# A top-2 expert layer on one core: tiles of two 128-slot halves, each with its own expert

## The chip, the core and the metric

The kernel runs on one core of a Trainium2 chip. The metric is the device time of one execution in microseconds (us). The engines are named as the profile names them: PE is TensorE, with its weight load as PEld, DVE is VectorE, ACT is ScalarE, POOL is GpSimd and SP is SyncE. A q behind a name (SPq, PEldq) is what that engine's sequencer does itself: register reads, waits, issues of DMAs.

## What is computed

The input x is 4 sequences of 1024 tokens of 128 numbers, all float32. Two blocks follow one another, each behind a layer norm with a shift, a scale and a gate drawn from a condition. The first is a scan over time: a small MLP is trained by one gradient step for each of 1024 time steps on all four sequences at once, and then applied to the queries. The second, which the change concerns, is a mixture of experts with 8 experts, 2 for each token, and a shared expert:

```python
def _L0_ffn_ref(x, w_router, W1, b1, W2, b2, Ws1, bs1, Ws2, bs2):
    D_MODEL, D_FF, N_EXPERTS, TOP_K, N_SHARED = (128, 512, 8, 2, 1)
    ...
    probs = jax.nn.softmax(logits, axis=-1)
    vals, idx = jax.lax.top_k(probs, TOP_K)
    gates = jnp.sum(jax.nn.one_hot(idx, N_EXPERTS, dtype=x.dtype) * vals[..., None], axis=-2)
    hs = jax.nn.gelu(jnp.einsum('btd,fd->btf', x, Ws1) + bs1)
    acc = jnp.einsum('btf,df->btd', hs, Ws2) + bs2
    h = jax.nn.gelu(jnp.einsum('btd,efd->btef', x, W1) + b1)
    y = jnp.einsum('btef,edf->bted', h, W2) + b2
    acc = acc + jnp.einsum('bted,bte->btd', y, gates)
    return SCALE * acc
```

## The kernel before

**Stages.** The scan (line 413 is the helper that records most of its matmuls) takes the first 345 us. From there to about 444 us come the queries, the second norm, the routing and the first 9 of 16 shared tiles. The rest, to about 620 us, is the stage of tiles. Last come the loads, sums and stores of the output.

**Tiles.** The 4096 tokens with 2 experts each make 8192 slots. They are sorted by expert into a DRAM array `xs` of 132-word rows (128 of the token, 4 of place and gate) by indirect DMAs that POOL issues. A tile is TS = 256 slots of one expert; since each expert's last tile may be part empty, the kernel runs the worst case, N_TILES = 39 tiles. DVE works out on the chip which expert tile j has (`e_i[j]`) and where it begins in `xs` (`row_i[j]`): for the first N_FULL = 9 tiles in `full_tiles`, from half of the routing alone, for the rest in `rest_marks`, `rest_experts` and `rest_rows` (lines 1832 to 1864). `table_ready` counts these tables.

**Jobs.** 39 expert tiles and the last 7 shared tiles make 46 jobs. In iteration i PE transposes the rows of job i+2 (`feed`, line 1424, 2 transposes), runs the first layer of job i+1 (`e_up`, line 1442, 4 matmuls of 256 columns into PSUM) and the second of job i (`e_down`, line 1456, 8 matmuls of 128 columns). A float32 matmul shows as two passes in the trace. ACT makes the gelu between the layers (line 1586, 4 instructions of 128x256). DVE copies the transposed rows out of PSUM (`hg`, line 1884), works out where each result row goes (`meta`, lines 1891 to 1897, 4 small operations), adds the bias (`yb`, line 1917) and multiplies by the gate (`yo`, line 1922). POOL writes `yo` to its places in DRAM (`ys`, line 2052).

**Loads.** SP issues both loads of a tile, in one queue: `weights(j)` brings both layers and biases of one expert (578 KB, `slab`, a ring of RW = 5) and waits until `yb` of tile j-5 is made; `rows(j)` brings the 256 rows (132 KB, `xt`, a ring of RX = 4). In the loop `weights(j)` follows `rows(j)`. At the turn to the later tiles SP waits for the second table, issues the weights of tiles 9 and 10, and only then the rows of tile 9. From tile LOAD_AT = 33 on it also issues the first loads of results, `yg`.

**End.** The output is finished in 8 groups of 512 tokens. `load(g)` brings a group's 512 KB of expert results; DVE sums it by three operations of 128x512 (`group_step`, lines 1871, 1874, 1878), and `store(g)` issues 4 stores. The eighth group is an exception: PE sums its two halves by matmuls with the identity (line 1531) and DVE needs two operations (lines 2012, 2016). SP stores the even groups, ACT the odd ones.

Of the kernel before, what the change touches and what calls it, by code (L numbers as in the profile page):

```python
# [10 lines left out]
I32 = mybir.dt.int32  # L11
# [20 lines left out]
SLAB = 2 * F + FT + D  # L32
N_TILES = (2 * B * S) // TS + E - 1
# [4 lines left out]
N_FULL = -(-(B * S - E * (TS - 1)) // TS)  # L38
EARLY_SH = 9
BY_HALF = -(-((B * S + E * (TS - 1)) // TS) * TS // TS)  # L40
BY_THREE = -(-((3 * B * S // 2 + E * (TS - 1)) // TS) * TS // TS)
# [8 lines left out]
XS_ROWS = -(-(E * CAP + (E - 1) * TS) // (8 * P)) * 8 * P  # L50
# [4 lines left out]
RW = 5  # L55
YS_ROWS = 2 * B * S + RY * TS
ROW = D + 4
N_TAB = E + E + E * E + CAP // TS + N_TILES + CH + SUB * RY + D


def program(nc, x, w_q, w_kv, w1, b1, w2, b2, w_router,
            s_w1t, s_b1, s_w2t, s_b2, cond, w_mod, slabs, ident_in, before_in, lower_in, tabs_in, xs, ys, out):
    with ExitStack() as ctx:
# [60 lines left out]
        etab = sb("etab", [P, N_TILES])  # L124
        e_i = sb("e_i", [P, N_TILES], I32)
        row_i = sb("row_i", [P, N_TILES], I32)
# [6 lines left out]
        for name, width in (("iota", E), ("down", E), ("tri", E * E), ("step", CAP // TS), ("tile", N_TILES), ("tau", CH), ("dump", SUB * RY), ("b2row", D)):  # L133
            cut[name] = tabs[:, at:at + width]
            at += width
# [1061 lines left out]
        with block() as blk:  # L1197
# [18 lines left out]
            over = psb("over", [P, E, CAP // TS])  # L1216
            tri = psb("tri", [P, 3 * E, E])
            past = psb("past", [P, N_FULL, E])
            full, number, weight = psb("full", [P, E]), psb("number", [P, 3 * E]), psb("weight", [P, 3 * E])
            first, rowf = psb("first", [P, N_TILES]), psb("rowf", [P, N_TILES])  # L1220
# [3 lines left out]
            slab = [psb(f"slab{i}", [P, SLAB]) for i in range(RW)]  # L1224
            hg = [psb(f"hg{i}", [P, TS]) for i in range(2)]
            hid = [psb(f"hid{i}", [P, FT, TS]) for i in range(2)]
# [3 lines left out]
            row2, rested = psb("row2", [P, SUB]), psb("rested", [P, 1408])  # L1230
# [19 lines left out]
            s_slab = [sem(f"s_slab{i}") for i in range(RW)]  # L1250
            meta_step, meta_ready = sem("meta_step"), sem("meta_ready")
            sum_ready, fin_ready, s_out = sem("sum_ready"), sem("fin_ready"), sem("s_out")
# [23 lines left out]
            def store(eng, g):  # L1276
                eng.wait_ge(fin_ready, g + 1)
                for b in range(B):
# [863 lines left out]
```

## Time and profile before

| What | Before |
|---|---|
| median of 3 runs | 635.91 us (635.18 to 636.79) |
| the profiled execution's own time | 635.87 us |
| span in its trace, first to last instruction | 634.1 us |
| mean granted TensorE clock | 0.967 |
| busy in the span: PE, PEld, DVE, ACT, POOL | 570.1, 512.1, 443.8, 333.6, 391.1 us |
| first layer of the expert tiles, L1442 | 312 passes, mean 380 ns |
| second layer, L1456 | 624 passes, mean 275 ns |
| weights of a tile, issue to landing | 39 loads of 578.0 KB, median 3.8 us |
| rows of a tile, issue to landing | 39 loads of 132.0 KB, median 3.2 us |
| results of a group, issue to landing | 8 loads of 512.0 KB, median 6.7 us |

The span leaves out 1.8 us of the execution's time. A pass of PE is listed with a duration that overlaps the next pass; how far the starts of passes are apart is read from the timeline. Idle time of an engine counts only where another engine waits for it.

### The profile page before, as it was taken

To read this page: it belongs to the slowest core of one execution; us is meant where nothing else is said; L and a number is where in the kernel's file an instruction comes from. 1 tells how busy PE (TensorE), PEld (TensorE's weight loads), DVE (VectorE), ACT (ScalarE), POOL (GpSimd) and SP (SyncE) were. 2 spreads that over 40 slices of the span, in tenths; PEclk is the share of its full clock that TensorE was granted. 3 is DMA by queue.
4 is the path that set the end of the run, shared out by engine and by line. 5 is a ranking of instruction groups with operands and counts; after the bars stand their busy time and mean duration, and the time that the engine had idled before them with its cause. 6 is when DMAs were issued, how large, how long until landed. Compare 5 with 4: busy or idle time off the path is not lost. (4 is left out here: it accounts for less than half of the span.)

```text
span 634.1 us, 14426 instructions
## 1 busy us (share of the span) xinstructions
PE 570.1 (90%) x4296; PEld 512.1 (81%) x4296; DVE 443.8 (70%) x1743; ACT 333.6 (53%) x1064; POOL 391.1 (62%) x598
## 2 busy tenths in 40 slices
PE   2469999999999999999996868789979999999993
PEld 2349999899999999999985557778869999999991
DVE  3736888888788888878886478884595465555765
ACT  2555666566566666656662374775434444444440
POOL 1525666656666665666652607888888886677760
PEclk9999999999999999999999768879999999999997
DMA  9079930000000000000000001145445577778945
GB/s 198 3 275 394 395 136 1 2 0 0 0 0 0 0 0 0 0 0 0 2 2 1 2 0 35 46 143 168 143 137 147 177 222 225 227 239 256 347 123 165
DMA packets 39796, 66.77 MB, mean 105 GB/s; under 512 B 7522, under 2 KB 26724, under 8 KB 39748
## 3 DMA queue, kind: packets, MB, share of 16 engines
q1 hardware_dynamic: 31076, 54.85, 27.4%
q0 software_dynamic: 4544, 9.45, 4.3%
q10 hardware_dynamic: 4128, 1.91, 1.4%
q8 instruction: 22, 0.36, 0.2%
q14 instruction: 26, 0.21, 0.1%
HBM read 36.26 MB, written 29.92 MB: 104 GB/s over the span
## 5 line engine op out<-in xcount | busy, mean ns | idle before, releaser
L1586 ACT ACTIVATE hid<-bank,slab 128x256 f32<-128x256 f32 x156 | 64.1, 470 | 85.1 <-PE bank L1442 85.0
L2052 POOL DMA_INDIRECT ys<-yo,dst x78 | 76.3, 979 | 36.8 <-DVE yo L1922 22.2
L2044 POOL DMA_INDIRECT xs<-hrow,slot_i x64 | 63.4, 990 | 35.8 <-issue 35.5
L1442 PE MATMUL bank<-hg,slab 128*128 128x256 f32 x312 | 73.9, 380 | 4.3 <-issue 3.9
L1456 PEld LDWEIGHTS bank<-slab,hid 128*128 128x128 f32 x624 | 75.8, 192 | 2.0
L1456 PE MATMUL bank<-slab,hid 128*128 128x128 f32 x624 | 76.0, 275 | 0.0
L1442 PEld LDWEIGHTS bank<-hg,slab 128*128 128x128 f32 x312 | 56.3, 190 | 11.0 <-issue 4.9
L1917 DVE TENSOR_TENSOR yb<-bank,slab 128x256 f32<-128x256 f32 x39 | 16.6, 424 | 61.9 <-PE bank L1456 61.7
L990 POOL TENSOR_TENSOR nL<-aL,ones 128x128 f32<-128x128 bf16 x32 | 16.9, 527 | 42.5 <-ACT aL L699 42.5
L413 PE MATMUL bank<-aH,W2p 128*128 128x128 f32 x192 | 42.4, 303 | 0.1
L413 PE MATMUL bank<-kv,W1b 128*128 128x128 f32 x192 | 41.4, 298 | 0.0
L1002 POOL TENSOR_TENSOR nH<-aH,ones 128x128 f32<-128x128 f32 x32 | 14.6, 455 | 36.7 <-ACT aH L717 36.7
L1922 DVE TENSOR_SCALAR yo<-yb,gt 128x128 f32<-128x128 f32 x78 | 34.3, 613 | 1.4
L2027 POOL MEMSET rested<- 128x1408 f32 x25 | 32.2, 1288 | 0.0
L413 PEld LDWEIGHTS bank<-aH,W2p 128*128 128x128 f32 x192 | 29.1, 191 | 3.4 <-DVE W2p L794 0.3
L413 PE MATMUL bank<-GX,ge 128*128 128x128 f32 x128 | 30.7, 322 | 0.6 <-DVE ge L794 0.5
L413 PEld LDWEIGHTS bank<-kv,W1b 128*128 128x128 f32 x192 | 29.8, 196 | 0.1
L994 POOL TENSOR_TENSOR oL<-tL,ones 128x128 f32<-128x128 f32 x32 | 14.5, 454 | 24.7 <-ACT tL L702 24.7
L1017 POOL TENSOR_TENSOR diff<-ge 128x256 f32<-128x256 f32 x32 | 23.3, 728 | 5.5 <-DVE sums L797 5.5
L794 DVE SCALAR_TENSOR_TENSOR gL<-qrowL,bank 128x128 bf16<-128x128 bf16 x64 | 18.4, 287 | 11.1 <-ACT qrowL L710 5.6
L974 POOL TENSOR_TENSOR GXb<-GX,ones 128x256 bf16<-128x256 f32 x32 | 23.3, 728 | 4.1 <-DVE GX L794 2.1
L413 PE MATMUL bank<-hT,wkv 128*128 (+1 forms) x128 | 23.6, 309 | 2.5 <-POOL arowL L1037 2.5
(353 smaller groups left out, 1882.4 us busy)
## 6 DMA issues: line engine op xcount, KB each, us to landing
slab<-in_slabs_dram SPq DMA_DIRECT2D x39, 578.0 KB, 3.8
xs<-fill SPq DMA_DIRECT2D x34, 528.0 KB
xt<-xs SPq DMA_DIRECT2D x39, 132.0 KB, 3.2
yg<-ys SPq DMA_DIRECT2D x8, 512.0 KB, 6.7
xr<-in_L_attn_x_dram SPq DMA_DIRECT2D x16, 128.0 KB, 7.0
ys<-yo,dst POOLq DMA_INDIRECT x78, 3.1
xs<-hrow,slot_i POOLq DMA_INDIRECT x64
out_dram<-xr SPq DMA_DIRECT2D x16, 64.0 KB, 2.9
```

Of the source, the lines that this page charges most:

```text
L413: return pe.matmul(dst, lhs, rhs, start=start, stop=stop, skip_group_check=True)
L794: return dve.scalar_tensor_tensor(out=dst, in0=a, scalar=s, in1=b, op0=o0, op1=o1)
L974: pool.tensor_tensor(GXb[r][:, :, :].rearrange("p k t -> p (k t)"), GX[r][:, :, :].rearrange("p k t -> p (k t)"), ones2[:, :], ALU.mult).t ...
L990: pool.tensor_tensor(nL[1][:, :], aL[1][:, :], ones2[:, 0:P], ALU.subtract).then_inc(l_n, 1)
L1017: pool.tensor_tensor(diff[:, :, :], ge[r % 2][1][:, :, :], ge[r % 2][0][:, :, :], ALU.subtract).then_inc(chk_d, 1)
L1442: mm = pe.matmul(e_half(i, n), left[:, n * P:(n + 1) * P], right, start=True, stop=True)
L1456: mm = pe.matmul(y[:, s * D:(s + 1) * D], hid[i % 2][:, n, s * P:(s + 1) * P], right, start=(n == 0), stop=(n == FT - 1), skip_group_check ...
L1586: nc.scalar.activation(hid[i % 2][:, n, :], e_half(i, n), ACT.Gelu_apprx_tanh, bias=bias).then_inc(e_x, 1)
L1922: dve.tensor_scalar(yo[v][:, s, :], yb[i % 2][:, s, :], gt[v][:, s:s + 1], None, ALU.mult).then_inc(e_yo, 1)
L2027: nc.gpsimd.memset(rested[:, :], 0.0).then_inc(pause_done, 1)
L2044: pool.indirect_dma_start(out=xs[:, :], out_offset=bass.IndirectOffsetOnAxis(ap=slot_i[:, i, c:c + 1], axis=0), in_=hrow[:, c, :], in_offs ...
L2052: pool.indirect_dma_start(out=ys[:, :], out_offset=bass.IndirectOffsetOnAxis(ap=dst[v][:, s:s + 1], axis=0), in_=yo[v][:, s, :], in_offset ...
```

## The change

The unit of routing becomes a half of 128 slots. A tile is still 256 slots wide, but its two halves may belong to different experts, and so the worst case is 72 halves or 36 tiles, 12 of them from the first half of the routing. What follows from this:

- `e_up` runs 8 matmuls of 128 columns, each half with its own weights; ACT runs 8 gelus of 128x128.
- The second layer's weights of all 8 experts, 2 MB, are loaded once into `w2` and stay. PE reads the two expert numbers of a tile into registers and addresses `w2` by them.
- SP brings two slabs of 128x644 (330 KB each, the first layer and biases) and two blocks of 128 rows (66 KB each) for a tile. For all but 6 tiles the slab's expert comes from the row number by a shift, without a read of `e_i`.
- The ring of slabs is 4 deep, not 5. The gelu writes into the buffers `hs` of the shared tiles.
- DVE's tables have 72 entries for 39, and their steps 128 for 256 slots; `meta` has 5 operations for 4.
- At the end DVE sums the eighth group too, by three operations; ACT issues its load, SP that of the seventh, and SP and ACT each issue half of its stores.

```diff
-SLAB = 2 * F + FT + D
-N_TILES = (2 * B * S) // TS + E - 1
+SLAB = F + FT + D
+HALF = P
+N_HALVES = -(-((2 * B * S) // HALF + E - 1) // SUB) * SUB
+N_TILES = N_HALVES // SUB
...
-RW = 5
+RW = 4
...
-            hid = [psb(f"hid{i}", [P, FT, TS]) for i in range(2)]
+            hid = hs
...
-                def weights(j):
+                def weights(j, experts):
                     if j >= RW:
                         sp.wait_ge(e_yb, job["expert", j - RW] + 1)
-                    e = sp.value_load(e_i[0:1, j:j + 1], min_val=0, max_val=E - 1)
-                    sp.dma_start(slab[j % RW][:, :], slabs[:, bass.ds(e, 1), :].rearrange("p o w -> p (o w)")).then_inc(s_slab[j % RW], 16)
+                    for s in range(SUB):
+                        sp.dma_start(slab[j % RW][:, s, :], slabs[:, bass.ds(experts[s], 1), :].rearrange("p o w -> p (o w)")).then_inc(s_slab[j % RW], 16)
+
+                def early_weights(j):
+                    weights(j, [sp.value_load(e_i[0:1, SUB * j + s:SUB * j + s + 1], min_val=0, max_val=E - 1) for s in range(SUB)])
...
+                    at = [sp.value_load(row_i[0:1, SUB * j + s:SUB * j + s + 1], min_val=0, max_val=XS_ROWS - HALF) for s in range(SUB)]
+                    for s in range(SUB):
+                        sp.dma_start(xt[j % RX][:, s, :], xs[bass.ds(at[s], HALF), :]).then_inc(s_xt[j % RX], 16)
...
                 for j in range(N_FULL, N_TILES):
-                    rows(j)
+                    at = rows(j)
                     if j >= N_FULL + 2:
-                        weights(j)
+                        weights(j, [a >> 12 for a in at])
...
                     for n in range(FT):
-                        mm = pe.matmul(e_half(i, n), left[:, n * P:(n + 1) * P], right, start=True, stop=True)
+                        if kind == "expert":
+                            for s in range(SUB):
+                                mm = pe.matmul(e_half(i, n)[:, s * P:(s + 1) * P], slab[j % RW][:, s, n * P:(n + 1) * P],
+                                               hg[j % 2][:, s * P:(s + 1) * P], start=True, stop=True)
...
+                        expert = [pe.value_load(e_i[0:1, SUB * j + s:SUB * j + s + 1], min_val=0, max_val=E - 1) for s in range(SUB)]
                     if i >= 2:
                         pe.wait_ge(e_yb, i - 1)
...
-                            right = slab[j % RW][:, F + n * P:F + (n + 1) * P] if kind == "expert" else sw[:, 1, n, :]
+                            right = w2[:, bass.ds(expert[s], 1), n * P:(n + 1) * P].rearrange("p o w -> p (o w)") if kind == "expert" else sw[:, 1, n, :]
...
-                pe.wait_ge(s_yg[NG - 1], 16)
-                for k in range(2):
-                    mm = pe.matmul(bank[7][:, :], ident[:, :], yg[NG - 1][:, :, k * D:(k + 1) * D], start=(k == 0), stop=(k == 1))
-                mm.then_inc(sum_ready, 1)
...
+                store(act, 1)
+                store(act, 3)
+                scattered(act, N_TILES)
+                load(act, 7)
+                store(act, 5)
+                store(act, 7, range(B // 2, B))
...
-                for k in range(18, 21):
+                for k in range(18, 24):
                     group_step(k)
```

Three places in the order of instructions follow. The semaphores in brackets carry reused names, which are given with each.

PE, one iteration in the stage of tiles, before. `h_U2` says that DVE has copied the fed rows out, `h_Tq` counts gelus and `h_T2` the `yb`s; the last named is the slab's load:

```order
1078 L1424 MATMUL bank<-ident,xt 128x128 [waits h_U2,s_xt0]
1079 L1424 MATMUL bank<-ident,xt 128x128
1080 L1442 MATMUL bank<-hg,slab 128x256 [waits h_Tq,h_U2,h_er2]
1081 L1442 MATMUL bank<-hg,slab 128x256 x3
1082 L1456 MATMUL bank<-slab,hid 128x128 [waits h_Tq,h_T2]
1083 L1456 MATMUL bank<-slab,hid 128x128 [waits h_Tq] x3
1084 L1456 MATMUL bank<-slab,hid 128x128 x4
```

The same iteration after, as far as the fourth instruction of the second layer. `h_U1` counts gelus, `h_Ta` the `yb`s, `h_W1` the copies; an ISA works on registers:

```order
1242 L1434 MATMUL bank<-ident,xt 128x128 [waits h_W1,s_xt2]
1243 L1434 MATMUL bank<-ident,xt 128x128
1244 L1453 MATMUL bank<-hg,slab 128x128 [waits h_U1,h_W1,h_gram]
1245 L1453 MATMUL bank<-hg,slab 128x128 x7
1246 L1469 TENSOR_LOAD e_i [waits table_ready]
1247 L1469 ISA x2
1248 L1469 TENSOR_LOAD e_i
1249 L1469 ISA x2
1250 L1477 ISA [waits h_U1,h_Ta]
1251 L1477 MATMUL bank<-w,hs 128x128
1252 L1477 ISA [waits h_U1]
1253 L1477 MATMUL bank<-w,hs 128x128
```

The second layer had its waits on its first matmuls. Now two reads of `e_i` stand behind the first layer, and each matmul has an address instruction ahead of it, the first four of which carry the waits.

SP, the turn to the later tiles, before. `h_T2` counts the `yb`s, `h_e` and `h_W1` free a block of rows:

```order
98 L1293 TENSOR_LOAD e_i [waits h_T2,table_ready]
99 L1293 ISA x2
100 L1294 ISA
101 L1294 DMA slab<-in_slabs_dram 128x1156
102 L1293 TENSOR_LOAD e_i [waits h_T2]
103 L1293 ISA x2
104 L1294 ISA
105 L1294 DMA slab<-in_slabs_dram 128x1156
106 L1300 TENSOR_LOAD row_i [waits h_e,h_W1,s_half1]
107 L1300 ISA x2
108 L1301 ISA
109 L1301 DMA xt<-xs 128x2x132
```

The same turn after, from the weights of tile 13 on (`h_Ta` counts the `yb`s, `h_W2` stands for `h_W1`):

```order
195 L1301 TENSOR_LOAD e_i
196 L1301 ISA x2
197 L1301 TENSOR_LOAD e_i
198 L1301 ISA x2
199 L1298 ISA [waits h_Ta]
200 L1298 DMA slab<-in_slabs_dram 128x644
201 L1298 ISA
202 L1298 DMA slab<-in_slabs_dram 128x644
203 L1307 TENSOR_LOAD row_i [waits h_e,h_W2,s_half1]
204 L1307 ISA x2
205 L1307 TENSOR_LOAD row_i
206 L1307 ISA x2
```

The rows of the first later tile stood behind the weights of tile 10, which wait for `yb` of tile 5; now they stand behind those of tile 13, which wait for `yb` of tile 9.

SP, one tile of the loop, before:

```order
182 L1293 TENSOR_LOAD e_i [waits h_T2]
183 L1293 ISA x2
184 L1294 ISA
185 L1294 DMA slab<-in_slabs_dram 128x1156
186 L1300 TENSOR_LOAD row_i [waits h_e,h_W1]
187 L1300 ISA x2
188 L1301 ISA
189 L1301 DMA xt<-xs 128x2x132
```

The same after, from the weights of one tile to the rows of the next:

```order
227 L1298 ISA [waits h_Ta]
228 L1298 DMA slab<-in_slabs_dram 128x644
229 L1298 ISA
230 L1298 DMA slab<-in_slabs_dram 128x644
231 L1307 TENSOR_LOAD row_i [waits h_e,h_W2]
232 L1307 ISA x2
233 L1307 TENSOR_LOAD row_i
234 L1307 ISA x2
235 L1309 ISA
236 L1309 DMA xt<-xs 128x132
237 L1309 ISA
238 L1309 DMA xt<-xs 128x132
```

Each tile now has two issues for one of either kind, and no read of `e_i`; two reads of `row_i` stand between the weights and the rows.

## Rows read from the trace of the kernel before

**Rows 1.** Busy time by window: stretch, length, engines' busy (instructions), PEclk, DMA share, GB/s

```profile
480.00:500.00 20.00, 20.00 (x142) 18.91 (x142) 9.44 (x29) 8.51 (x21) 16.40 (x17) 1.00 0.64 193
...
580.00:600.00 20.00, 20.00 (x144) 18.97 (x143) 12.38 (x46) 8.83 (x22) 14.30 (x14) 1.00 0.99 329
600.00:620.00 20.00, 20.00 (x142) 18.79 (x140) 14.32 (x37) 8.21 (x20) 12.17 (x12) 1.00 0.51 158
620.00:634.00 14.00, 3.86 (x5) 1.18 (x4) 6.90 (x11) 0.00 (x0) 0.00 (x0) 0.72 0.57 163
```

**Rows 2.** Timeline of PE, one job: start, duration, line, count of passes

```profile
503.00 0.38 PE L1424 MATMUL bank<-ident,xt 128*128 128x128 f32 x2
503.22 1.89 PE L1442 MATMUL bank<-hg,slab 128*128 128x256 f32 x8
...
506.74 0.38 PE L1424 MATMUL bank<-ident,xt 128*128 128x128 f32 x2
```

**Rows 3.** Timeline of PE: its two idle gaps, in brackets, in the stage of tiles

```profile
467.47 1.96 PE L1442 MATMUL bank<-hg,slab 128*128 128x256 f32 x8 [1.41 <-issue]
...
473.73 1.97 PE L1442 MATMUL bank<-hg,slab 128*128 128x256 f32 x8 [2.51 <-issue]
```

**Rows 4.** Timeline of DVE, operations of the tables

```profile
455.85 0.55 DVE L1832 TENSOR_TENSOR xn<-held,tabs 128x384 f32<-128x384 f32 x1
...
464.48 0.90 DVE L1848 TENSOR_TENSOR xn<-tabs,last 128x720 f32<-128x720 f32 x1
```

**Rows 5.** Register reads by line: duration ns min/median/max, first and last start

```profile
L1101 PEldq TENSOR_LOAD <-count x1: 490/490/490, 348.9 to 348.9; - x1
...
L1293 SPq TENSOR_LOAD <-e_i x39: 264/309/526, 420.8 to 597.0; - x39
L1293 SPq FUSED_REGOPS  x39: 147/147/154, 421.1 to 597.4; - x39
...
L1454 PEldq EVENT_SEMAPHORE  x2: 51/51/51, 502.4 to 505.9; - x2
```

**Rows 6.** Timeline of PE in the stage of shared tiles

```profile
415.36 0.23 PE L1382 MATMUL bank<-selb,lowerb 128*128 128x64 bf16 x1 [2.94 <-DVE selb L1746]
415.41 0.45 PE L1386 MATMUL bank<-selb,onesq 128*128 128x64 bf16 x8
415.72 3.76 PE L1415 MATMUL bank<-sw,hs 128*128 128x128 f32 x16
419.27 2.92 PE L1398 MATMUL bank<-hT,sw 128*128 128x256 f32 x8
...
422.90 1.95 PE L1415 MATMUL bank<-sw,hs 128*128 128x128 f32 x16
```

**Rows 7.** Timelines of DVE, SP and PE around one load of rows

```profile
533.13 0.42 DVE L1917 TENSOR_TENSOR yb<-bank,slab 128x256 f32<-128x256 f32 x1 [1.93 <-PE bank L1456]
...
534.32 0.35 SPq L1294 DMA_DIRECT2D slab<-in_slabs_dram  x1
535.49 0.37 SPq L1301 DMA_DIRECT2D xt<-xs  x1
...
544.05 0.38 PE L1424 MATMUL bank<-ident,xt 128*128 128x128 f32 x2
```

**Rows 8.** Landing of the loads of rows: 16 from 521 to 577 us, 5 from 580 us

```profile
DMA to landing us min/median/max: 3.0/3.2/3.5
...
DMA to landing us min/median/max: 6.2/6.7/7.2
```

**Rows 9.** Timeline of the end, SP, DVE and PE

```profile
620.14 0.82 SPq L1274 DMA_DIRECT2D yg<-ys  x2
...
624.03 0.69 DVE L1871 TENSOR_TENSOR ysum<-yg 128x512 f32<-128x512 f32 x1 [0.37 <-DMA yg<-ys]
...
625.31 3.78 PE L1531 MATMUL bank<-yg,ident 128*128 128x512 f32 x4 [5.23 <-DMA yg<-ys]
...
629.86 0.69 DVE L2016 TENSOR_TENSOR xr<-ysum,xr 128x512 f32<-128x512 f32 x1
```

More of the change, by code:

```diff
@@ L132, in program @@
         at = 0
-        for name, width in (("iota", E), ("down", E), ("tri", E * E), ("step", CAP // TS), ("tile", N_TILES), ("tau", CH), ("dump", SUB * RY), ("b2row", D)):
+        for name, width in (("iota", E), ("down", E), ("tri", E * E), ("step", CAP // HALF), ("tile", N_HALVES), ("tau", CH), ("dump", SUB * RY), ("b2row", D)):
             cut[name] = tabs[:, at:at + width]
@@ L1223, in program @@
             xt = [psb(f"xt{i}", [P, SUB, ROW]) for i in range(RX)]
-            slab = [psb(f"slab{i}", [P, SLAB]) for i in range(RW)]
+            slab = [psb(f"slab{i}", [P, SUB, SLAB]) for i in range(RW)]
+            w2 = psb("w2", [P, E, F])
             hg = [psb(f"hg{i}", [P, TS]) for i in range(2)]
-            hid = [psb(f"hid{i}", [P, FT, TS]) for i in range(2)]
+            hid = hs
             yb = [psb(f"yb{i}", [P, SUB, D]) for i in range(2)]
@@ L1274, in load, with store @@
                 eng.dma_start(yg[g][:, :, :], ys_v[:, g * GRP:(g + 1) * GRP, :]).then_inc(s_yg[g], 16)
-            def store(eng, g):
+            def store(eng, g, bs=range(B)):
                 eng.wait_ge(fin_ready, g + 1)
-                for b in range(B):
+                for b in bs:
                     eng.dma_start(out_v[b][:, g * GRP:(g + 1) * GRP, :],
@@ L1329, in _ @@
                 load(sp, 6)
-                load(sp, 7)
                 store(sp, 4)
                 store(sp, 6)
+                store(sp, 7, range(0, B // 2))
                 sp.wait_ge(s_out, 16 * B * NG)
@@ L1419, in feed @@
                 def feed(j):
-                    pe.wait_ge(s_xt[j % RX], 16 * (j // RX + 1))
+                    pe.wait_ge(s_xt[j % RX], 16 * SUB * (j // RX + 1))
                     if j >= 2:
@@ L1441, in e_up @@
                     for n in range(FT):
-                        mm = pe.matmul(e_half(i, n), left[:, n * P:(n + 1) * P], right, start=True, stop=True)
+                        if kind == "expert":
+                            for s in range(SUB):
+                                mm = pe.matmul(e_half(i, n)[:, s * P:(s + 1) * P], slab[j % RW][:, s, n * P:(n + 1) * P],
+                                               hg[j % 2][:, s * P:(s + 1) * P], start=True, stop=True)
+                        else:
+                            mm = pe.matmul(e_half(i, n), left[:, n * P:(n + 1) * P], right, start=True, stop=True)
                         if n % 2:
@@ L1641, in _ @@
                     e_gelu(i)
-                for g in range(1, NG, 2):
-                    store(act, g)
+                store(act, 1)
[4 more added lines that the diff above has]
+                store(act, 7, range(B // 2, B))
             @blk.vector
```

120 lines of the change are left out of this document (62 added, 58 removed).

## Prediction

> **What bounds the kernel now.** I read the windows first, for the engine that is never idle. From 480 to 620 us there are seven windows of 20 us, and PE is busy for all 20.00 in each, at a granted clock of 1.00; two of them and the last stand in [rows 1]. Every other engine has room, DVE 14.32 at most, and the DMA share reaches 0.99 in one window only. So a microsecond of PE's work in the stage of tiles is a microsecond of time, unless something else becomes late. After 620 us PE does 3.86 us of work in 14, and the end is a chain of load, sum and store. The timeline of PE gives the price of a job [rows 2]: feed to feed, 506.74 - 503.00 = 3.74 us. The feed takes 0.22 of it, to the first layer's start, and the two layers share the other 3.52. Sixteen narrow passes are listed with 1.95 [rows 6], the last with some 0.275 of its own (the mean in the table), so 15 starts fill 1.675 us: a pass of 128 columns is 0.112, sixteen are 1.79, and the first layer's 8 passes of 256 have the other 1.73, 0.216 each. Once the first jobs are through, only two gaps break the stage, 1.41 and 2.51 us, both of PE waiting for DVE, which is busy with the tables of the later tiles [rows 3].
>
> All sums are made against the profiled execution, 635.87 us (span 634.1 and 1.8 outside it), which is the median, 635.91, within 0.04.
>
> **Fewer tiles.** 39 tiles become 36: 3 x 3.74 = 11.2 us off PE's path. **-11.2**, with nothing to hide it, since PE is the bound.
>
> **Narrower first layer.** 16 passes of 0.112 replace 8 of 0.216: 1.79 against 1.73, 0.06 a tile, 36 x 0.06 = **+2.2**. ACT's 8 gelus for 4 lie beside PE and cost nothing: ACT is busy for 8 to 9 us in 20 [rows 1], and even if each half took as long as a whole, twice that is 18. If that cover is gone, the second layer waits.
>
> **Register reads on PE.** They are new. A read with its two register steps took SP 0.31 + 0.15 us at the median of 39, 0.53 + 0.15 at most; the only one that PE's sequencer makes took 0.49 [rows 5]. Two reads, their steps and small gaps come to some 1.1 to 1.6 us. What hides them is the queue between the sequencer and the array: the wait of a second layer was taken at 505.9 [rows 5], while its passes begin one period and one first layer after 503.22 [rows 2], at 508.7. That is 2.8 us ahead: 8 passes of 256 columns, 2 of the feed and some 7 of the second layer before, about 17. After the change the passes behind which the reads stand are the 16 narrow ones, so the cover is about 1.8 us, and the reads fit. The address step ahead of each matmul is not the limit either: 8 matmuls with 8 weight loads went out in 0.3 us [rows 6], so a matmul of two passes with one more step needs less than its 0.22. Term **0**, ends 0 and +3.6 (0.1 us in each of 36 tiles); beyond that it is a rival, below.
>
> The Trainium skill (Advanced Engine Details and Errata, Engine Queue Depths) gives TensorE a queue of 64. By it, even if a pass takes two places, 32 x 0.112 = 3.6 us of work would cover the reads, and no rival would be left there. The trace disagrees: the lead is about 17 passes.
>
> **DVE's tables.** An operation over 384 numbers takes 0.55 us and one over 720 takes 0.90 [rows 4], about 1.04 ns a number. The two over 384 get 768 numbers (0.95, so +0.8 in all), the four over 720 get 48 x 24 = 1152 (1.35, so 4 x 0.45 = +1.8). The first two stand in a stretch where PE didn't wait; the four stand ahead of the copies for which PE waits in [rows 3], so the gaps grow by their sum. **+1.8**, ends +0.6 and +2.6. A fifth operation in `meta` is some 0.1 us of an idle engine.
>
> **The turn to the later tiles.** The rows of tile 12 now stand in SP's queue behind the weights of tile 13, which wait for `yb` of tile 9. PE wants them one job of 3.6 us (no feed in it) after it ends that tile's second layer. Until they are there: 0.5 for `yb` [rows 7], 0.3 to SP's answer, 0.85 for two issues of 0.35 and their address steps, 1.0 for two reads with their steps [rows 5], 0.4 for the second issue's turn, 2.5 for landing (below the 3.2 of twice as much, [rows 8]). That is 5.6, and PE waits **+2.0**, ends 0 and +3.
>
> **Slack of the rows in the loop.** Before, `yb` ends at 533.55, the slab is issued at 534.32, the rows at 535.49, they land 3.2 later at 538.7, and the feed comes at 544.05: 5.3 us to spare [rows 7, 8]. With a ring of 4 the `yb` waited for is one period later (-3.74), two issues and a read replace one each (+0.5 in net, as SP's read of `e_i` goes), and the second block lands some 0.6 sooner: 1.7 us are left. In the undisturbed stretch that is enough, though SP then issues for about 3.5 of 3.8 us. When the result loads start, at 580 us and after, the rows land after 6.2 to 7.2 us [rows 8], 4.0 more than 3.2. The slack is outrun by 4.0 - 1.7 = 2.3. PE's being late then gives the next four tiles their slack back. **+2.3**, ends 0 and +4.6 (twice).
>
> **The end.** DVE sums the eighth group itself. Before, that load landed at 625.3, PE took 3.8, DVE ended at 629.86 + 0.69 = 630.55 [rows 9]. After, the loads of groups 7 and 8 start together on two queues. If the seventh still lands at 624.0, six operations of 0.72 end at 628.3 (-2.2). The last group's four stores, 0.4 to 0.5 us apart, become two on each queue, -1.0 more. **-3.2** at best. The DMA share in that stretch is near 1 already, and two loads that run at once may both land at 625.0 to 625.3; then the sum ends at 629.3 to 629.6. I take **-2.3**.
>
> On this the Trainium skill (Trainium Kernel Development and Optimization, Key Constraints) says that all queues run on the same 16 DMA engines, and issuing from several saves only the issue time. By it the second queue is worth the 0.4 us between two issues and the end -2.3, not -3.2; the trace of before has one queue there and can't tell.
>
> **The clock.** In the stage of shared tiles PE's clock fell to the lower of its levels when PE had idled 2.94 us; the next 16 + 8 passes took 3.76 + 2.92 us where 1.95 + 1.89 is normal, so a fall costs 2.8 us [rows 2, 6]. After a gap of 2.51 it didn't fall [rows 3]. The gaps to come are 2.3 and 3.4 us on DVE, 2.0 at the turn and 2.3 late. I take half a fall, **+1.4**, ends 0 and +5.6.
>
> **Sum.** -11.2 + 2.2 + 0 + 1.8 + 2.0 + 2.3 - 2.3 + 1.4 = -3.8: 635.9 - 3.8 = **632.1 us**. This case spans 629.0 to 634.0.
>
> **Rivals.**
> - *Clean.* The new gaps don't appear: rows land sooner at half the size, and SP keeps ahead. For it: 1.7 us of slack in the middle, and 600 to 620 us with a DMA share of 0.51. Against it: the landing of 7 us. -11.2 + 2.2 + 1.8 - 3.2 = -10.4: **625.5**. Chance 0.18.
> - *Gaps breed.* The transfers outrun the ring more than once and the clock falls twice: +4.6 for 2.3 and +5.6 for 1.4 would give 638.6; one of the two doubled gives **634 to 637.8**, no change that can be told. For it: SP is filled to nine tenths, so that it can't catch up quickly. Chance 0.20.
> - *PE's reads outlast the queue* (the other side). The pair of reads stands on PE in every expert tile. It decides from 1.8 us, 0.8 for each read with its steps; PE's own read took 0.49 where SP's median is 0.31, so it is not far. At 2.0 us each tile loses 0.2: 36 x 0.2 = +7.2, so 632.1 + 7.2 = **639.3**. If a read waits until the array has emptied, the whole pair of 1.3 us shows, and 36 x 1.3 = +47 gives 679. Chance 0.17, of which 0.04 for the second.
> - *The change doesn't do what it says.* The 36 tiles are a constant of the program, so the count can't fail; the second queue can (the end -2.3, in the sum).
>
> **Chances.** The forecast has 0.45. A measurement of this kernel can tell about 0.3%, 1.9 us, from no change, so faster means below 634.0 and slower above 637.8. Faster: 0.45 + 0.18 = 0.63. Same: 0.20. Slower: 0.17. The range takes in the clean case and reaches past 637.8 for part of the reads: 624.8 to 638.4.
>
> **What the profile after would show.** PE's job in the undisturbed middle: 3.80 us from feed to feed if the reads are hidden, 4.0 or more with idle time put down to the issue ahead of the second layer if not. The wait ahead of the second layer stays about 1 us ahead of its passes. Two gaps of PE before 480 us, of 2.3 and 3.4. One gap of 2 us ahead of the feed of tile 12, and one or two ahead of feeds after the first result loads; their releaser is the load of rows. The granted clock says what they cost. At the end no matmul after 620 us, and DVE ending some 8 us after the two loads' issue. I am wrong if the period is far from 3.8, or if the gaps are ahead of other instructions than these.

## Result and the profile after

The changed kernel took 646.11 us (median of 4, 644.02 to 649.87) against 635.97 (4 runs, 635.18 to 636.79): a ratio of 1.0149, with an interval of 1.011 to 1.0187. The forecast was 632.1, faster, with a range to 638.4. So both the direction and the range were missed. Ratios, here and below, are taken over each kernel's fast runs alone, so they aren't exactly the quotients of the medians beside them.

| | before | after |
|---|---|---|
| span of the traced execution | 634.1 us | 644.5 us |
| first feed of the stage of tiles | 444.64 | 442.26 |
| start of the last run of second-layer passes | 616.34 | 628.21 |
| stage of tiles, between these two | 171.7 | 186.0 |
| from there to the end | 17.8 | 16.3 |

The page of after, the share of the engines and the issues of the two loads:

```profile
PE 564.6 (88%) x4502; PEld 513.4 (80%) x4502; DVE 440.4 (68%) x1756; ACT 349.3 (54%) x1196; POOL 384.4 (60%) x591
...
slab<-in_slabs_dram SPq DMA_DIRECT2D x72, 322.0 KB
xt<-xs SPq DMA_DIRECT2D x72, 66.0 KB
```

The same windows as in [rows 1], with the one in which tile 12 comes (columns as there):

```profile
480.00:500.00 20.00, 20.00 (x164) 19.46 (x164) 8.10 (x38) 8.91 (x30) 16.46 (x17) 1.00 0.53 157
500.00:520.00 20.00, 15.23 (x114) 14.09 (x113) 6.26 (x29) 8.74 (x32) 14.19 (x14) 0.88 0.52 160
580.00:600.00 20.00, 17.89 (x154) 17.32 (x155) 10.41 (x45) 11.99 (x44) 12.38 (x13) 1.00 0.79 239
600.00:620.00 20.00, 17.44 (x153) 16.87 (x152) 12.25 (x44) 10.00 (x36) 10.97 (x11) 1.00 0.96 310
```

In [rows 1] PE is busy for the whole of each window of 20 us. Now only the window from 480 us is full: 15.2 us are busy from 500, and 17.9 and 17.4 at the end. Between 580 and 600 us the DMA engines are less busy than before (0.79 for 0.99), so what PE lacks there isn't their bandwidth, which points to loads that are issued late. From 600 us they carry what they did earlier before (0.96 for 0.51).

The stage grew by 14.3 us where the forecast's terms give -1.5. The first answer is the view of PE's waits in that stage: what waited, for what, us in total, times, longest (the lines of the feed and the first layer).

```profile
PE bank L1434 <- DMA xt<-xs: 7.9, 5, 4.4
PE bank L1453 <- issue: 7.3, 4, 2.7
PE bank L1434 <- issue: 1.1, 1, 1.1
```

L1434 is the feed, L1453 the first layer of an expert tile, L1477 the second. Before, PE waited for no load of rows at all. The timeline of PE shows where (start, duration, line, passes; idle time ahead and what ended it in brackets):

```profile
468.14 0.38 PE L1434 MATMUL bank<-ident,xt 128*128 128x128 f32 x2
471.01 3.56 PE L1453 MATMUL bank<-hg,slab 128*128 128x128 f32 x16 [2.49 <-issue]
...
511.26 1.95 PE L1477 MATMUL bank<-w,hs 128*128 x16
517.56 0.69 PE L1434 MATMUL bank<-ident,xt 128*128 128x128 f32 x2 [4.35 <-DMA xt<-xs]
518.04 3.62 PE L1456 MATMUL bank<-hT,sw 128*128 128x256 f32 x8
...
527.31 0.38 PE L1434 MATMUL bank<-ident,xt 128*128 128x128 f32 x2
...
531.10 0.38 PE L1434 MATMUL bank<-ident,xt 128*128 128x128 f32 x2
...
546.49 2.33 PE L1453 MATMUL bank<-hg,slab 128*128 128x128 f32 x16
548.98 2.12 PE L1477 MATMUL bank<-w,hs 128*128 x16 [0.16 <-issue]
...
597.16 0.44 PE L1434 MATMUL bank<-ident,xt 128*128 128x128 f32 x2 [0.98 <-DMA xt<-xs]
...
602.35 0.44 PE L1434 MATMUL bank<-ident,xt 128*128 128x128 f32 x2 [1.18 <-DMA xt<-xs]
```

Where nothing disturbs it a job takes 531.10 - 527.31 = 3.79 us, as forecast, against 3.74 in [rows 2]. Going through the timeline and taking from each piece what it takes undisturbed (0.22, 1.79, 1.79) leaves what the stage lost:

| Lost by PE in the stage of tiles | before | after | forecast of the growth |
|---|---|---|---|
| waits behind DVE's tables, 454 to 480 us | 4.2 | 7.3 | +1.8 |
| rows of tile 12, at the turn | 0 | 4.5 | +2.0 |
| feeds ahead of the result loads, from 589 us | 0 | 5.3 | +2.3 |
| small pieces in between | 0 | 4.2 | 0 |
| passes at the lower clock | 0 | 5.5 | +1.4 |

SP issues all the loads, so its register reads come next. The view by line, of before and of after: duration in ns min/median/max.

```profile
L1300 SPq SEQ_ASSERT  x39: 18/18/18, 435.0 to 594.9; - x39
```

```profile
L1307 SPq TENSOR_LOAD <-row_i x72: 3/267/691, 431.8 to 609.6; - x72
L1307 SPq FUSED_REGOPS  x72: 3/152/689, 432.1 to 609.9; - x72
L1307 SPq SEQ_ASSERT  x72: 2/18/679, 432.3 to 610.1; - x72
```

A check of a register takes 18 ns at each of its 39 places before, and up to 679 ns after. Such a break of up to 0.7 us falls on any of SP's instructions, whatever it does. Counted in the records of SP between 415 and 613 us, an instruction or a gap without a wait that is about 0.3 us or more too long stands there 78 times after and 6 times before, where most are at an issue of a DMA. The lengths of the 78 add up to 46 us, but that is not time lost: the records that follow are too short. 150 of SP's 726 records there last 2 to 15 ns, and before, where the shortest is 17 ns, none does. Taken from one wait to the next, SP's stretches in the trace of after are 18 us longer in all than the same stretches usually are in the two later traces of this kernel without breaks (e10 and e15, themselves 7 and 5 us over by the same count). No other engine's sequencer shows records of this kind; PE's is late in another way, below. The medians, on which my sum rested, did not move.

### The profile page after: what moved, and what is told of

Same layout as the page of the kernel before. It is cut to its first block and busy times, and to the rows that moved or that the text cites. A ratio compares the mean times of both kernels' runs of the same rounds, so it can differ in the third digit from the quotient of the medians.

```text
span 644.5 us, 15675 instructions
## 1 busy us (share of the span) xinstructions
PE 564.6 (88%) x4502; PEld 513.4 (80%) x4502; DVE 440.4 (68%) x1756; ACT 349.3 (54%) x1196; POOL 384.4 (60%) x591
## 3 DMA queue, kind: packets, MB, share of 16 engines
q1 hardware_dynamic: 35732, 56.29, 28.1%
## 5 line engine op out<-in xcount | busy, mean ns | idle before, releaser
L2070 POOL DMA_INDIRECT ys<-yo,dst x72 | 69.7, 968 | 56.7 <-DVE yo L1947 42.3
L1603 ACT ACTIVATE hs<-bank,slab 128x128 f32<-128x128 f32 x144 | 55.9, 388 | 84.5 <-PE bank L1453 47.4
L1453 PE MATMUL bank<-hg,slab 128*128 128x128 f32 x576 | 73.3, 281 | 7.6 <-issue 7.3
L1453 PEld LDWEIGHTS bank<-hg,slab 128*128 128x128 f32 x576 | 69.2, 196 | 9.2 <-issue 8.9
L1477 PE MATMUL bank<-w,hs 128*128 x576 | 72.7, 280 | 1.0 <-ACT hs L1605 0.7
L1477 PEld LDWEIGHTS bank<-w,hs 128*128 128x128 f32 x576 | 69.8, 196 | 2.4 <-issue 1.9
L1942 DVE TENSOR_TENSOR yb<-bank,slab 128x256 f32<-128x256 f32 x36 | 15.3, 425 | 73.9 <-PE bank L1477 60.1
L1605 ACT ACTIVATE hs<-bank,slab 128x128 f32<-128x128 f32 x144 | 56.5, 392 | 0.0
```

What stands on the lines that cost most here:

```text
L1453: mm = pe.matmul(e_half(i, n)[:, s * P:(s + 1) * P], slab[j % RW][:, s, n * P:(n + 1) * P], hg[j % 2][:, s * P:(s + 1) * P], start=True, s ...
L1477: mm = pe.matmul(y[:, s * D:(s + 1) * D], hid[i % 2][:, n, s * P:(s + 1) * P], right, start=(n == 0), stop=(n == FT - 1), skip_group_check ...
L1603: nc.scalar.activation(hid[i % 2][:, n, 0:P], e_half(i, n)[:, 0:P], ACT.Gelu_apprx_tanh, bias=slab[j % RW][:, 0, F + n:F + n + 1])
L1605: nc.scalar.activation(hid[i % 2][:, n, P:TS], e_half(i, n)[:, P:TS], ACT.Gelu_apprx_tanh, bias=slab[j % RW][:, 1, F + n:F + n + 1]).then_ ...
L2070: pool.indirect_dma_start(out=ys[:, :], out_offset=bass.IndirectOffsetOnAxis(ap=dst[v][:, s:s + 1], axis=0), in_=yo[v][:, s, :], in_offset ...
```

## The experiments

There were two questions: which part of the change makes the loads late, and where the breaks come from. Runs that stand together ran on one chip. "Lost" is the stage of tiles less what its passes take undisturbed: 166.9 us with the wide first layer (39 x 0.22 + 46 x 1.73 + 44 x 1.79), 157.9 with the narrow one (36 x 0.22 + 36 x 1.79 + 7 x 1.73 + 41 x 1.79). It is 4.8 before and 28.1 after. (The expectations use an earlier count, up to 2 us higher for the wide kernels and up to 1 us lower for the narrow ones.) "Breaks" gives their number and the sum of their lengths, without what the short records after them give back.

### One chip: ring, turn, issues, end

e1, a ring of 5:

```diff
-RY = 10
-RW = 4
+RY = 7
+RW = 5
```

> The changed kernel with a ring of 5 slabs instead of 4; to make room, the ring of result buffers goes from 10 to 7. The computation is whole. If the ring of 4 is what makes PE late in the middle (excesses of 0.4 to 0.8 us at 501, 546, 563 and 579 us, 4.3 in all) and late (five gaps ahead of feeds, 5.3 in all), both go, and the time falls by some 9 us, to 637. If SP itself is too slow, a deeper ring helps only where SP waited for yb: the late gaps shrink and the gap of 4.4 at the turn stays: 640 to 643. If the ring of 10 for results mattered, it is slower.

e2, the turn:

```diff
-                early_weights(N_FULL)
-                early_weights(N_FULL + 1)
                 sp.wait_ge(s_half[1], 16 * CH)
                 for j in range(N_FULL, N_TILES):
                     at = rows(j)
-                    if j >= N_FULL + 2:
-                        weights(j, [a >> 12 for a in at])
+                    weights(j, [a >> 12 for a in at])
```

> The changed kernel with one thing moved in SP's order: at the turn to the later tiles the rows of tile 12 and then its weights are issued, instead of the weights of tiles 12 and 13 ahead of its rows. The computation is whole. If the gap of 4.35 us ahead of the feed of tile 12 comes from the weights ahead in SP's queue, it goes, and with it the 2.1 us for the fall of the clock behind it: 646.1 - 6.5 = 639.6. If it comes from stalls of SP's own, most of it stays and the time is 644 or more.

e3, the kernel before with twice the issues:

```diff
-                    sp.dma_start(slab[j % RW][:, :], slabs[:, bass.ds(e, 1), :]...
+                    for h in range(2):
+                        sp.dma_start(slab[j % RW][:, h * (SLAB // 2):(h + 1) * (SLAB // 2)], ...
...
+                    at = [sp.value_load(row_i[0:1, j:j + 1], min_val=0, max_val=XS_ROWS - TS) for s in range(SUB)]
+                    for s in range(SUB):
+                        sp.dma_start(xt[j % RX][:, s, :], xs[bass.ds(at[s] + s * P, P), :]).then_inc(s_xt[j % RX], 16)
```

> The kernel before, where SP issues each load of weights as two halves of the columns and each load of rows as two blocks of 128, the second with a row read of its own. The computation is whole. SP then has some 16 instructions a tile instead of 8. In the trace of before no register or address instruction of SP takes over 0.6 us; in the trace of after some 75 take about 0.7 us, 50 us in all. If the number of instructions that SP must get through without a rest brings these stalls, they appear here too, tens of them; whether the time moves depends on the ring of 5 (5.3 us to spare): 636 to 638. If they come from something else in the change (the shift of a register, the resident weights, PE's reads), there are none here.

e4, the kernel before with the new end alone, as in the part on the end of the change's diff:

> The kernel before with the end of the changed one alone: the eighth group's load by ACT, its sum by three operations of DVE, its stores from both queues. The computation is whole. Forecast from the rows -2.3 us, -3.2 at best: 632.7 to 633.6. In the trace of after the stretch from the last pass of the second layer to the end is 12.6 us where it was 14.0 before, which would give -1.4: 634.5. If the second queue or DVE's share of the end costs more than PE's sum did, the time is 636 or more.

| Run | median us | ratio to before there | stage | lost | breaks of SP (us) |
|---|---|---|---|---|---|
| before (13 runs) | 638.70 | | | | |
| e1 | 646.55 | 1.0137 (1.0085 to 1.019) | 179.1 | 21.2 | 91 (57) |
| e2 | 649.78 | 1.0191 (1.014 to 1.0243) | 182.8 | 24.9 | 91 (56) |
| e3 | 651.67 | 1.023 (1.0177 to 1.0283) | 189.4 | 22.5 | 97 (56) |
| e4 | 636.80 | 0.9991 (0.9962 to 1.002) | 175.0 | 8.1 | 80 (47) |

e3 is the telling one: the old kernel, with 39 tiles, the ring of 5 and the old tables, becomes 2.3% slower when SP's issues and its reads of rows are doubled. PE waits for rows 9 times in it, 10.5 us in all; in e4 once, 0.2 us. e4 is the other half: the same breaks, 80 of them, in the old instruction stream of SP, cost 2 to 3 us of the stage (175.0, for 171.7 to 173.0 in the traces of before without breaks). So the breaks aren't made by the change, and under them dense work on SP has a price. What it costs without them is not known for this kernel, as e3 ran on this chip alone. e1 took 7 us off the stage, as a deeper ring should: PE's waits for rows fell from 7.9 us to 0.6 in the view of its waits, 2.6 with two late feeds for whose wait the view finds no releaser. It did not take them off the time, because its stage began at 451.1 instead of 442.3; a part of each comparison is decided before the stage begins. In e2 the feed of tile 12, at 519.12, doesn't wait at all, where 4.5 us were lost ahead of it, and the stage is 3.2 us shorter:

```profile
510.00 1.92 PE L1474 MATMUL bank<-w,hs 128*128 x15 [1.00 <-issue]
...
519.12 0.38 PE L1431 MATMUL bank<-ident,xt 128*128 128x128 f32 x2
```

The gap at 510.00 stands inside a second layer, not ahead of a feed; it is the 1.2 us (with the passes' own spacing) that the expectation of e13 takes for the rest of the turn.

e4 also measures the end: no gain that can be told.

### A second chip: before again, PE's reads, ring of 4, shared work

e5 is the kernel before once more. e7 replaces PE's reads in the changed kernel, so that the second layer takes the wrong experts' weights, with the same amount of work:

```diff
-                        expert = [pe.value_load(e_i[0:1, SUB * j + s:SUB * j + s + 1], min_val=0, max_val=E - 1) for s in range(SUB)]
+                        expert = [(2 * j + s) % E for s in range(SUB)]
```

e8 takes a buffer of weights from the kernel before:

```diff
-RW = 5
+RW = 4
```

e9 has the edit of e2 and gives each of SP and ACT one half of a tile; ACT issues after the gelus of tile j:

```diff
                 for i in range(len(JOBS)):
                     e_gelu(i)
+                    kind, j = JOBS[i]
+                    if kind == "expert":
+                        if j + 4 < N_TILES:
...
+                            known[j + 4] = rows(act, j + 4, [1])
+                        if 4 <= j + 3 < N_TILES:
+                            weights(act, j + 3, known.pop(j + 3))
```

> The kernel before once more, for its trace. In the first trace of it SP's sequencer runs without a break between 415 and 613 us; in the traces of the four runs so far, one of which has the same instructions of SP as before up to 600 us, single register, address and issue instructions of SP take 0.7 us, some 60 to 90 times. If these breaks are something that comes and goes from execution to execution, this trace may show them, and the span then tells what they cost the kernel before: with 5.3 us of slack under 4 us. If they hang on the program, this trace has none, like the first.

> The changed kernel, where PE reads no expert number and addresses the resident second-layer weights by fixed numbers (2j and 2j+1, modulo 8), so that the second layer uses the wrong expert's weights; all amounts of work are the same. If the reads and address steps are hidden by the queue ahead of the array, as forecast, the time stays at 646 within 1.5 us. If they cost PE after each late load, when the queue has run empty (0.1 to 0.4 us seen ahead of the second layer), it falls by 1 to 3 us. If they cost in each tile it falls by 4 us or more.

> The kernel before with a ring of 4 slabs instead of 5, nothing else. The computation is whole. By the slack of 5.3 us less one period, 1.6 us are left; if the ring is what makes PE late in the changed kernel, this shows gaps of about 1 us ahead of feeds once the result loads start and small ones before: +3 to +8, 640 to 644. If SP's number of instructions is what matters and not the ring, it stays within 2 us of before.

> The changed kernel with SP's work shared: from tile 4 on SP issues the rows and weights of the first half of a tile and ACT those of the second, each with one register read and two issues a tile; at the turn the rows come first. The computation is whole. If SP's load of instructions, about 3.5 of 3.8 us a tile plus its breaks, is what delays the loads, the gap at the turn, those in the middle and the late ones (4.5 + 4.2 + 5.3 = 14 us of PE's time) mostly go: 633 to 638, about the time of before or below. If the DMA engines or the ring are what delays them, it stays at 643 or more. If ACT, with 2.0 us of gelus and 1.4 us of issues a tile, becomes late, PE waits for gelus ahead of the second layer instead.

| Run | median us | ratio to before there | stage | lost | breaks of SP (us) |
|---|---|---|---|---|---|
| before (25 runs) | 634.65 | | | | |
| e5, before | 630.01 (1 run) | | 173.0 | 6.1 | 6 (5) |
| e7 | 630.52 | 0.9958 (0.9906 to 1.001) | 175.7 | 17.8 | 9 (10) |
| e8 | 634.89 | 1.0032 (0.998 to 1.0083) | 176.1 | 9.2 | 0 |
| e9 | 628.14 | 0.9909 (0.9858 to 0.996) | 165.8 | 7.9 | 7 (5) |

The breaks were gone, in the kernel before and in the three others. That made e7 unreadable by itself: 0.996 for 1.015 could be the reads or the chip. So the changed kernel had to run again beside it.

### A third chip: the changed kernel itself

> The changed kernel again, unaltered. The traces so far fall in two kinds: in five of them, among them the first of the changed kernel, SP's sequencer breaks off for 0.7 us some 80 to 95 times between 415 and 613 us; in five others, among them both of the kernel before and the one with SP's work shared, hardly ever. If the breaks are what cost the changed kernel its gain, a trace without them shows the middle free of gaps and an excess of PE in the stage of tiles of some 15 us instead of 27, and the ratio to before is 0.995 to 1.000; a trace with them repeats 1.015. If the cause is in the program, the ratio is 1.015 either way.

> The kernel with fixed expert numbers on PE (the second layer uses the wrong expert's weights) again, beside the changed kernel itself. The first time it came out at 0.996 of before, in a trace with no breaks of SP. If PE's reads cost nothing, it is within 1.5 us of the run of the changed kernel beside it; if they cost, it is faster by 3 us or more.

> The kernel with SP's work shared with ACT again, beside the changed kernel itself. The first time it came out at 0.991 of before, in a trace with no breaks of SP. If SP's load matters even without breaks, it is faster than the changed kernel by the gap at the turn and the late gaps, 3 to 7 us; with breaks in the trace by 10 or more.

> The changed kernel with the rows of tile 12 ahead of its weights at the turn, again, beside the changed kernel. The first time, in a trace full of breaks, the gap ahead of the feed of tile 12 was 1.2 instead of 4.5 us, but the whole was not faster. If the order at the turn matters without breaks, the gap of about 2 us and some of the clock's fall go: faster by 2 to 4 us than the changed kernel; if not, within 1.5.

| Run | median us | ratio to before there | stage | lost | breaks of SP (us) |
|---|---|---|---|---|---|
| before (31 runs) | 634.71 | | | | |
| e10, the changed kernel | 632.37 | 0.9964 (0.9927 to 1.0) | 172.6 | 14.7 | 11 (10) |
| e11, as e7 | 629.68 | 0.9961 (0.9913 to 1.001) | 171.0 | 13.1 | 9 (9) |
| e12, as e9 | 629.94 | 0.9946 (0.9899 to 0.9992) | 167.8 | 9.9 | 3 (2) |
| e13, as e2 | 631.18 | 0.9941 (0.9881 to 1.0001) | 167.9 | 10.0 | 14 (10) |

Without the breaks the same program loses 14.7 us instead of 28.1. SP's reads and PE's waits in e10:

```profile
L1307 SPq TENSOR_LOAD <-row_i x72: 260/268/524, 434.7 to 596.2; - x72
L1307 SPq SEQ_ASSERT  x72: 18/18/18, 435.2 to 596.7; - x72
```

```profile
PE bank L1434 <- DMA xt<-xs: 5.9, 4, 3.5
PE bank L1453 <- issue: 3.4, 2, 2.3
```

The 7.9 us for rows are 5.9, the 7.3 ahead of first layers 3.4, and the small pieces in the middle have gone. The second of these differences isn't the breaks': e15, the same kernel without breaks, waits 7.1 us there. PE's reads cost nothing that can be told here: e11 and e10 have the same ratio. e13 and e12 take a further 5 us off the stage.

### Program or moment

> The kernel before again, for a trace beside those of the next two. If breaks of SP's sequencer appear in this call's traces, they are in this one too, and then the slack of 5.3 us swallows them: PE's excess in the stage of tiles stays below 11 us. If this trace has none while the changed kernel's beside it has 60 or more, the breaks hang on the changed program and not on the chip or the moment.

> The changed kernel a third time, beside the kernel before and the one with SP's work shared. With breaks of SP in the trace: about 1.5% above before, PE's excess 25 us or more. Without: 0.996 of before and 15 us, as the second time.

> The kernel with SP's work shared with ACT a third time. If breaks appear in this call and SP's slack is what they eat, this kernel loses at most 3 to 5 us to them where the changed kernel loses 14, since SP then has half the issues and reads to do; without breaks it repeats 0.991 to 0.995 of before.

These ran on the second chip again, and had no breaks (5, 7 and 7). Before was 636.59 in one run (630.72 over 19), the changed kernel 631.70 (ratio 1.0007, 0.9964 to 1.0049; stage 173.2, lost 15.3) and the shared one 626.37 (0.9933, 0.989 to 0.9976; stage 167.6, lost 9.8). The last three ran on a fourth chip:

> The kernel before, for a trace. If SP's breaks appear in this call, the theory of slack says PE's excess in the stage of tiles stays below 11 us here, as in the kernel before with the new end (9.8 with 80 breaks).

> The changed kernel beside it. With breaks: 1.015 of before and PE's excess 25 us or more. Without: 0.996 to 1.001, excess 15 us.

> The kernel with SP's work shared with ACT. If SP's breaks appear in this call: PE's excess in the stage of tiles below 14 us and a ratio to before of 1.000 or less, since SP has half the issues; if it is 1.01 or more, SP's load is not what makes the changed kernel pay. Without breaks it repeats 0.991 to 0.995.

| Run | median us | ratio to before there | stage | lost | breaks of SP (us) |
|---|---|---|---|---|---|
| e17, before | 636.13 (1 run; 637.15 over 7) | | 174.1 | 7.2 | 75 (46) |
| e18, the changed kernel | 650.84 | 1.021 (1.0181 to 1.0238) | 187.0 | 29.1 | 79 (49) |
| e19, as e9 | 644.78 | 1.0105 (1.0078 to 1.0133) | 186.4 | 28.6 | 46 (27) |

Here they were again, in all three, the kernel before too. Its row of the same check:

```profile
L1300 SPq SEQ_ASSERT  x39: 3/18/726, 433.5 to 595.9; - x39
```

So the breaks belong to the chip or the moment, not to the program: of the experiments' traces seven on two chips had them (e1 to e4, e17 to e19), eleven on two others did not, and each chip was all of one kind. The first pair, on which the result rests, is mixed: without them before, with them after. The slack that I had read for the kernel before is real: 75 and 80 breaks cost its stage 1 to 3 us (e17, e4, beside before, e5 and e14), while the stage of the changed kernel is about 14 us longer with 79 of them (e18 beside e10 and e15).

The DMA packets of these traces show what a break is worth. In before, e5 and e14 the first packet of a load of weights starts 0.97 to 0.98 us (medians) after the start of its issue, which lasts 346 ns. In e17 it is 0.97 or 0.98 us behind ten of the eleven issues of that length, but behind the eleven that last 3 to 15 ns it starts between 0.18 us before and 0.82 us after the record: there the record is late, and the issue was made earlier than it says. The loads are late all the same. From the end of the `yb` that frees a slab to the first packet of its load, e17 takes 2.4 us at the median, the three others 1.7 to 1.8. So a break delays SP, by less than the records say: counted from wait to wait, SP is 20 us over in e17, 19 in e18 and 16 in e19, against 2 in before.

What fell is my remedy, and with it the view that SP's load is what the changed kernel pays for: the expectation of e19 made 1.01 or more the sign of that, and it came to 1.0105. e19 has some 60% of SP's instructions and 46 breaks for 79, and its stage is as long as e18's; of the 4.9 us between the two traces only 0.6 lie in the stage. PE's waits of e18 and then of e19 show what happened:

```profile
PE bank L1434 <- DMA xt<-xs: 8.1, 4, 3.7
PE bank L1453 <- issue: 7.2, 7, 3.7
```

```profile
PE bank L1450 <- issue: 10.9, 6, 3.3
PE bank L1474 <- ACT hs L1602: 2.8, 5, 0.7
PE bank L1431 <- DMA xt<-xs: 2.5, 1, 2.5
```

The wait for rows went from 8.1 to 2.5 us, as it should. But waits ahead of the first layer (L1450 there) rose from 7.2 to 10.9, of which 8.1 are behind DVE's tables, and waits for gelus grew. A part of the rest is PE's own sequencer. In the trace of after the small pieces of the middle stand at 546.5, 562.7 and 579.1, 16 us apart, in e18 at 548.6, 565.0 and 581.1, in e19 at 546.8, 563.1 and 579.3. The timeline of e18 at one of them:

```profile
548.64 0.83 PE L1453 MATMUL bank<-hg,slab 128*128 128x128 f32 x6
549.65 1.36 PE L1453 MATMUL bank<-hg,slab 128*128 128x128 f32 x10 [0.18 <-issue]
551.28 1.94 PE L1477 MATMUL bank<-w,hs 128*128 x15 [0.27 <-issue]
```

The array runs dry in the middle of one first layer, with no semaphore there. From its wait ahead of a first layer to the first read of `e_i` PE's sequencer takes at most 1.2 us in each tile between 524 and 590 us in the six traces without breaks that have narrow passes and these reads (e9, e10, e12, e13, e15, e16). In each of the five with breaks (after, e1, e2, e18, e19) it takes 1.4 us or more three or four times, with 3.3 us at most; after has 1.74 ending at 527.3, 1.45 at 547.5, 2.31 at 563.8 and 2.02 at 580.0. So PE's sequencer too is late in the traces with breaks, and PE stands still for it. The kernels with wide passes (e4, e17) show no such piece; the 2.8 us that their sequencer is ahead would cover it. Whether PE's instructions and SP's come late for one reason, and what a break is, no run shows.

## Why the prediction was wrong

**Fewer tiles, narrower first layer.** Right: 3.79 us a job, and no job's passes were slower but by the clock.

**Register reads on PE.** Right where nothing disturbs, by the row of after that answers to [rows 5] (same columns):

```profile
L1469 PEldq TENSOR_LOAD <-e_i x72: 293/300/539, 445.0 to 622.5; - x72
```

They are hidden, and removing them changed nothing that can be told (e10 beside e11). The term of 0 failed with the breaks, some 3 us in the small pieces: PE's sequencer was then late by more than the cover of 1.8 us. The rival named the thin cover, and put the cause in the read's own length, which was wrong.

**DVE's tables.** +1.8 forecast. The operations over many numbers took what was forecast (1.35 us over 1152). e10 lost 3.7 us there against 4.2 before, but after lost 7.3 and e15, without breaks, 7.6. In these two the small operations on the way were long as well: three that take 0.74 us together in e10 took 2.52, two took 2.05 (2.04 in e15) for 0.57, one 1.76 for 0.27. Each stretch ends within 0.1 us of the end of an operation of POOL over it, in after two on the shared bias and one filling `rested`. The forecast had no term for that, and it isn't the breaks'.

```profile
461.09 2.52 DVE L1867 TENSOR_TENSOR tri<-number,tabs 128x64 f32<-128x64 f32 x3
```

```profile
462.24 1.28 POOL L2051 TENSOR_TENSOR xr<-xr,gsb 128x512 f32<-128x512 f32 x1
...
469.01 1.27 POOL L2051 TENSOR_TENSOR xr<-xr,gsb 128x512 f32<-128x512 f32 x1
```

**The turn.** The place and the chain were right, the size too small even undisturbed: 3.6 us in e10 and 2.6 in e15 for 2.0. In after it was 4.5. It is the order in SP's queue: with the rows first, nothing of it is left in e2 and e13.

**Slack of the rows.** This is the step that failed, and the term of 0 for PE's reads with it. "In the undisturbed stretch that is enough, though SP then issues for about 3.5 of 3.8 us" was worked out from medians of a trace in which SP was never late. Undisturbed it held: nothing was lost between 525 and 580 us in e10, and 3.2 us late, for 2.3. But I left 0.3 us in 3.8 for anything else on SP and 1.8 us of cover for PE, and in the measured execution both sequencers were late. Against the forecast the rows cost 9.8 us at the turn and late (4.3), the small pieces 4.2 (0), the clock behind the gaps 5.5 (1.4) and DVE's stretch +3.1 (+1.8); that is 15.1 of the 15.8 us by which the stage missed. How much of it is SP's is not shown. Rows made PE wait 7.9 and 8.1 us with breaks and 5.9 and 4.7 without (after and e18; e10 and e15), 2 to 3.4 us more, and e19, with SP relieved, lost as much as e18. The rest is PE's sequencer in part, the clock in part, and open in part.

The ring, to which I gave the loss of slack, has its part too: the ring of 4 alone lengthened the stage of the kernel before to 176.1 us, from 171.7 to 173.0 in its traces without breaks (e8, ratio 1.0032 with an interval that takes in 1), and the ring of 5 took PE's waits for rows under breaks from 7.9 to 2.6 at most (e1).

**The end.** -2.3 forecast. The timeline of e10 shows the new end, to be laid beside [rows 9]:

```profile
620.32 0.34 SPq L1278 DMA_DIRECT2D yg<-ys  x1
620.62 0.39 ACTq L1278 DMA_DIRECT2D yg<-ys  x1
...
624.65 0.69 DVE L1897 TENSOR_TENSOR ysum<-yg 128x512 f32<-128x512 f32 x1 [2.12 <-DMA yg<-ys]
...
628.15 0.69 DVE L1904 TENSOR_TENSOR xr<-ysum,xr 128x512 f32<-128x512 f32 x1
```

DVE does both groups from the landing on, back to back. Over 14 traces with the new end the stretch from the last run of second-layer passes takes 16.3 us on the mean, over the 6 with the old one 17.6: -1.3. Both loads land together, as the bound for -2.3 had it. But e4, the one trace that has the new end and nothing else new, takes 17.4, and its time could not tell the gain from zero. So the end itself is worth 0.2 us as far as is shown, and the rest of the -1.3 is not explained.

**The clock.** I took half a fall, +1.4; after had 5.5 us of it, after gaps of 2.65, 2.49 and 4.35. The gap of 2.49 was followed by passes at the lower level, 16 in 3.56 us, where 2.51 in [rows 3] was not. e10 had 3.4 us of it. It follows from the gaps being more and longer.

**The range** went wrong with that step. Every term's upper end assumed sequencers that keep their medians, and even all upper ends together, with the end at -2.3, give 644.0; the chance of 0.17 for slower hung on the length of PE's reads alone. Without breaks the forecast of 0.994 was met nearly once (0.9964) and missed once (1.0007); with them it was missed by far (1.0149 and 1.021).

**A better version** came out where there are no breaks: with SP's work shared and the rows first at the turn, 0.9909, 0.9946 and 0.9933 of before on two chips, each interval below 1. The rows first alone (e13) give as short a stage, 167.9 for 167.8 (e12). The shared work is not better everywhere: 1.0105 on the chip with breaks.

## To carry to other kernels

A queue that is to be filled to nine tenths by a change has no room for what the trace at hand does not happen to show; price it by what it costs when the queue stands still for a microsecond, and ask who has that slack. A record that is too long is not yet time lost: add the short ones behind it, and look when the packets start. Where fewer but denser steps replace idle ones, compare the slack, not only the work. And a difference of 1% between two traces may be the chip's: run both kernels together, on more than one.

## What was not expected

- SP's records can be up to 0.7 us too long, 75 to 97 times in 200 us (46 to 57 us in all, of which some 20 are left when the short records behind them are counted), on some chips and not on others, with the same program; and PE's sequencer is late in the same traces.
- The kernel before has no single time. Over 25 runs on the second chip it took 627.4 to 636.6 us, in clusters near 628, 630 and 635.5. The traces of it begin the stage of tiles at 437.75 (e5), 442.67 (e17), 444.64 and 445.06 us (e14), and the stages that follow differ by 2.4 us only. What decides it in the stage of shared tiles was not looked into.
